# Turning the activations with DMA transposes in a fused conditional-mix and quantized-FFN kernel

## The chip, the cores and the metric

The kernel runs on one core of a Trainium2 chip. The metric is the device time of one execution in microseconds; lower is better. The kernel before was timed three times: 110.67, 111.22 and 111.39 us, median 111.22 us.

## The reference

```
w   = cond_weights[itok]                        # gather: 64 rows of a [200, 64, 64] table
y   = einsum('bct,bcd->bdt', x, w)              # x is [64, 64, 512] f32
a   = mxfp4_quant_dequant(y)                    # blocks of 32 along the 512 columns
W   = mxfp4_quant_dequant(ffn_weight)           # [512, 512]
out = x + (a @ W.T + bias)
```

`mxfp4_quant_dequant` takes the largest magnitude of each block of 32, makes a power-of-two scale from its exponent, rounds the scaled values to the e2m1 grid and scales back. All values that it gives are exact in bf16.

## The kernel before, in words

**Tiling.** Two batches of x make one tile of 128 partitions by 512 columns (32 tiles). Four tiles make a group; the code calls the work on a group a step, and there are 8 steps (`STEPS = LAST = 8`). Step 0 stands for the weight W, which goes through the same quantization.

**What one step does.** TensorE multiplies each x tile with a block-diagonal 128x128 matrix `mix` (`mix_tile`, line 252; two table rows are loaded into its diagonal blocks by `load_mixes`, line 157, one DMA of 16 KB for each) into PSUM `y_ps`. ScalarE reads y twice: magnitudes to `z` in bf16 (`z_tile`, line 356) and the value to `y_sb` in f32 (`y_tile`, line 364). VectorE reduces z to a block maximum (lines 460 to 477), makes the grid's scales from it (483 to 504, the last of them `inv`), rounds (`round_y`, line 512), limits (`limit`, line 524, which needs ScalarE's `zone`, line 372) and rescales to the quantized bf16 activations `a2` (`rescale`, line 533). The matmul with W needs the activations with k on the partitions. So TensorE transposes a2 with an identity matrix, 16 blocks of 128x128 a step (`turn_tile`, line 265), into the banks of `o_ps`; ScalarE copies them to `aT` in SBUF (`copy_turned`, line 389), and TensorE multiplies (`ffn_tile`, line 276, after a bias matmul of three partitions, `bias_tile`, line 270). Of the four output tiles in `o_ps`, tile 0 is added to x by VectorE (`add_residual`, line 538) and tiles 1 to 3 are copied by ScalarE to `o_sb` (`copy_out`, line 380) and added to x by an accumulating DMA that GpSimd issues (line 235). In the last two steps VectorE adds all tiles.

**What sets the order.** There is no planner; each engine's program is a list written out by hand, run strictly in order, with semaphore waits. The engines are skewed: in the VectorE loop (lines 579 to 594) iteration `step` rounds and rescales group `step`, begins the maxima of group `step+1`, and between them adds tile 0 of group `step-1`. TensorE in iteration `step` multiplies group `step-1` with W, mixes group `step+2` and turns group `step`.

**The queues.** SP issues in this order: the list of conditions, x of group 1 in two halves, the second half of W, then for each group the table rows of its tiles 2 and 3 and an x load of 1 MB, down to group 8 (lines 172 to 187); only behind that come the stores of each group, each behind the wait for its sums (lines 189 to 198). GpSimd issues the bias load, the table rows of tiles 0 and 1, splits the bias into three bf16 parts (lines 218 to 224), spreads them by four DMAs (227), and then issues the accumulating DMAs. ScalarE issues the first half of W.

**The start.** VectorE clears part of `mix`, quantizes W (lines 547 to 567), then begins group 1. TensorE turns W before it mixes group 2, and ScalarE copies the turned W to `wT` (line 410) before it makes zone of group 1. TensorE runs 72 small matmuls on zeros at the very start (line 291).

Of the kernel before, what the change touches and what calls it, by code (L numbers as in the profile page):

```python
# [13 lines left out]
P = 128  # L14
# [20 lines left out]
def adaln_ffn_program(nc, x, cond, table, W, bias, out):  # L35
# [11 lines left out]
    with ExitStack() as ctx:  # L47
# [13 lines left out]
        aT = sb("aT", [P, GROUP, KC, P], BF16)  # L61
# [6 lines left out]
        bias_f = sb("bias_f", [1, 3, N], F32)  # L68
# [24 lines left out]
        upper_clear, lower_clear = sem("upper_clear"), sem("lower_clear")  # L93
# [47 lines left out]
        def o_bank(step, t):  # L141
            if step < LAST or t >= 2:
                return o_ps[:, t if step < LAST else t - 2, :]
            return y_ps[:, 2 + t, :]
# [16 lines left out]
        def _(sp):  # L161
# [41 lines left out]
        def _(pool):  # L203
            nc.gpsimd.memset(mix[C:P, 0:GROUP, 0:C], 0.0).then_inc(lower_clear, 1)
            pool.dma_start(bias_f[:, 0, :], bias.rearrange("(o n) -> o n", o=1)).then_inc(bias_in, 16)
            pool.wait_ge(cond_in, 16)
            load_mixes(pool, mybir.EngineType.Pool, pool_mix_in, 1, POOL_TILES)
            pool.wait_ge(lower_clear, 1)
            nc.gpsimd.memset(mix[C:P, GROUP:TILES, 0:C], 0.0).then_inc(lower_clear, 1)
            pool.wait_ge(lower_clear, 2)  # L210
            pool.wait_ge(ident_clear, 1)
            nc.gpsimd.affine_select(out=ident[:, :], in_=ident[:, :], compare_op=ALU.not_equal, fill=1.0,
                                    base=0, pattern=[[-1, P]], channel_multiplier=1).then_inc(ident_ready, 1)
            load_mixes(pool, mybir.EngineType.Pool, pool_mix_in, 2, POOL_TILES)


            pool.wait_ge(bias_in, 16)
            nc.gpsimd.tensor_copy(bias_b[:, 0, :], bias_f[:, 0, :]).then_inc(bias_step, 1)
            for i in range(2):
                pool.wait_ge(bias_step, 2 * i + 1)  # L220
                nc.gpsimd.tensor_tensor(bias_f[:, i + 1, :], bias_f[:, i, :], bias_b[:, i, :], ALU.subtract
                                        ).then_inc(bias_step, 1)
                pool.wait_ge(bias_step, 2 * i + 2)
                nc.gpsimd.tensor_copy(bias_b[:, i + 1, :], bias_f[:, i + 1, :]).then_inc(bias_step, 1)
            pool.wait_ge(bias_step, 5)
# [3 lines left out]
            for step in range(3, STEPS + 1):  # L229
                load_mixes(pool, mybir.EngineType.Pool, pool_mix_in, step, POOL_TILES)  # L230
# [8 lines left out]
        def _(pe):  # L239
# [15 lines left out]
            def turn_tile(step, t):  # L255
                if step == 1:
                    pe.wait_ge(wT_copied, t + 1)
                elif 1 < step < LAST:

                    if t < ADDED:  # L260
                        pe.wait_ge(added, adds_before(step - 1) + t + 1)
                    else:
                        pe.wait_ge(copied_out, (GROUP - ADDED) * (step - 2) + t - ADDED + 1)
# [5 lines left out]
            def bias_tile(step, t):  # L269
                nc.tensor.matmul(o_bank(step, t), ones[32 * t:32 * t + 3, :], bias3[32 * t:32 * t + 3, :],  # L270
                                 start=True, stop=False)

            def ffn_tile(step, t):
                pe.wait_ge(aT_ready, tiles_done(step, t))
                for c in range(KC):
                    last = nc.tensor.matmul(o_bank(step, t), aT[:, t, c, :], wT[:, c, :], start=False,  # L276
                                            stop=(c == KC - 1))
                last.then_inc(o_ready, 1)

            def ffn_group(step):  # L280

                pe.wait_ge(aT_ready, tiles_done(step, GROUP - 1))
# [10 lines left out]
            pe.wait_ge(upper_clear, 1)  # L293
# [8 lines left out]
            for t in range(GROUP):  # L302
                mix_tile(2, t)
            for step in range(1, LAST):
                if step == 2:
                    pe.wait_ge(ones_ready, 1)
                    pe.wait_ge(bias3_in, 16 * GROUP)
                if step > 1:
# [4 lines left out]
                for t in range(GROUP):  # L313
                    turn_tile(step, t)
# [4 lines left out]
            pe.wait_ge(aT_ready, tiles_done(LAST - 1, GROUP - 1))  # L319
# [18 lines left out]
            pe.wait_ge(added, adds_before(LAST - 1) + 2)  # L338
# [6 lines left out]
        def _(act):  # L345
# [36 lines left out]
            def copy_turned(step, t, n):  # L382

                act.wait_ge(t_ready, GROUP * step + (t + n if step < LAST else t // 2 * 2 + 2))
                if step < LAST:
                    turned = o_ps[:, t:t + n, :].bitcast(BF16)[:, :, 0:K]
                else:
                    turned = y_ps[:, t // 2, :].bitcast(BF16).rearrange("p (g k) -> p g k", k=K)[:, t % 2:t % 2 + n, :]
                nc.scalar.copy(aT[:, t:t + n, :, :].rearrange("p g c m -> p g (c m)"), turned).then_inc(aT_ready, n)  # L389
# [8 lines left out]
            for t in range(GROUP):  # L398
                z_tile(1, t)
                if t > 0:  # L400
                    y_tile(1, t - 1)
            y_tile(1, GROUP - 1)
            for t in range(GROUP):
                z_tile(2, t)
                if t > 0:
                    y_tile(2, t - 1)
# [5 lines left out]
            for step in range(1, LAST):  # L412
                zone_group(step)
                if step == 1:
                    y_tile(2, 3)
                else:
                    if step + 1 <= LAST:
# [8 lines left out]
                copy_turned(step, 0, 2)  # L426
                copy_turned(step, 2, 2)
# [11 lines left out]
        def _(dve):  # L439
# [104 lines left out]
            nc.vector.memset(mix[0:C, :, C:P], 0.0).then_inc(upper_clear, 1)  # L544
# [80 lines left out]
```

## Time and profile before

| | |
|---|---|
| median of the three runs | 111.22 us |
| the profiled execution, its own time | 110.9 us |
| its span in the trace | 109.2 us |
| VectorE (DVE) busy | 92.5 us |
| TensorE (PE) busy | 80.3 us |
| ScalarE (ACT) busy | 79.0 us |
| GpSimd (POOL) busy | 34.3 us |
| mean granted TensorE clock | 0.937 of full speed |

PE is TensorE's matmuls, PEld its weight loads, SPq, POOLq and ACTq are DMA issues on those engines' queues. A line number is a line of the kernel. Times are in microseconds from the start of the span; the profiled execution has 1.7 us that lie outside the span.

### The profile page before, as it was taken

To read this page: it belongs to the slowest core of one execution; us is meant where nothing else is said; L and a number is where in the kernel's file an instruction comes from. 1 tells how busy PE (TensorE), PEld (TensorE's weight loads), DVE (VectorE), ACT (ScalarE), POOL (GpSimd) and SP (SyncE) were. 2 spreads that over 40 slices of the span, in tenths; PEclk is the share of its full clock that TensorE was granted. 3 is DMA by queue.
4 is the path that set the end of the run, shared out by engine and by line. 5 is a ranking of instruction groups with operands and counts; after the bars stand their busy time and mean duration, and the time that the engine had idled before them with its cause. 6 is when DMAs were issued, how large, how long until landed. Compare 5 with 4: busy or idle time off the path is not lost.

```text
span 109.2 us, 1704 instructions
## 1 busy us (share of the span) xinstructions
PE 80.3 (74%) x440; PEld 39.9 (37%) x440; DVE 92.5 (85%) x145; ACT 79.0 (72%) x113; POOL 34.3 (31%) x55
## 2 busy tenths in 40 slices
PE   5994900299140999799969969997996994389960
PEld 4952200363010834263443435335353341324420
DVE  5245999999509986999999999999999999999970
ACT  3433298006993559999999999999999999873300
POOL 4393999846754475130030003003001100300000
PEclk9999998558985589999999999999999999999999
DMA  1996989979597510339389596938948777694995
GB/s 38 401 372 136 301 304 394 332 214 357 186 295 260 192 35 22 119 76 199 101 304 180 108 362 130 180 141 285 196 113 327 144 144 285 171 207 134 350 385 203
DMA packets 13850, 23.70 MB, mean 217 GB/s; under 512 B 3846, under 2 KB 4370, under 8 KB 13842
## 3 DMA queue, kind: packets, MB, share of 16 engines
q1 hardware_dynamic: 11506, 17.83, 46.7%
q0 software_dynamic: 2048, 5.26, 23.7%
q10 hardware_dynamic: 288, 0.52, 1.3%
q8 instruction: 3, 0.05, 0.2%
q14 instruction: 5, 0.04, 0.1%
HBM read 10.49 MB, written 8.39 MB: 173 GB/s over the span
## 4 chain that ended last, share of the span: by engine, by line
DVE 59%; PE 16%; ACT 9%; issue 6%; DMA 5%; SPq 2%; DVEq 0%; ACTq 0%
DVE n_int L512 11%; DVE top L524 10%; DVE a L533 10%; DVE low L499 7%; PE y_ps L252 6%; DMA w_sb<-in_L_ffn_weight_dram 5%; DVE inv L504 4%; PE o_ps L265 3%; DVE n_int L517 3%; PE o_ps L276 3%; ACT zone L372 3%; DVE m L460 3%; DVE amax L477 2%; DVE m L466 2%; DVE s L483 2%
## 5 line engine op out<-in xcount | busy, mean ns | idle before, releaser
L252 PE MATMUL y_ps<-x_sb,mix 128*128 128x512 f32 x64 | 32.6, 639 | 4.1 <-DMA mix<-in_L_cond_weights_dram 4.1
L276 PE MATMUL o_ps<-wT,aT 128*128 128x512 bf16 x120 | 27.5, 380 | 0.0
L356 ACT ACTIVATE z<-y_ps 128x512 bf16<-128x512 bf16 x32 | 19.1, 621 | 8.4 <-PE y_ps L252 7.8
L265 PE MATMUL o_ps<-ident,a 128*128 128x128 bf16 x128 | 10.2, 242 | 17.6 <-DVE a L533 17.6
L157 POOL DMA_DIRECT2D mix<-in_L_cond_weights_dram x32 | 17.4, 546 | 13.2 <-issue 11.9
L372 ACT ACTIVATE zone<-inv 128x2048 int16<-128x2048 int16 (+1 forms) x10 | 17.5, 1755 | 3.8 <-DVE inv L504 3.7
L512 DVE TENSOR_TENSOR n_int<-y_sb,inv 128x1024 int16<-128x1024 f32 x16 | 19.0, 1222 | 0.8
L235 POOL DMA_DIRECT2D x_sb<-o_sb x6 | 5.3, 882 | 44.8 <-ACT o_sb L380 44.8
L364 ACT COPY y_sb<-y_ps 128x512 f32<-128x512 f32 x32 | 18.5, 607 | 0.0
L252 PEld LDWEIGHTS y_ps<-x_sb,mix 128*128 128x128 f32 x64 | 12.4, 207 | 15.8 <-issue 15.0
L265 PEld LDWEIGHTS o_ps<-ident,a 128*128 128x128 bf16 x128 | 8.6, 109 | 23.9 <-DVE a L533 15.5
L276 PEld LDWEIGHTS o_ps<-wT,aT 128*128 128x128 bf16 x120 | 11.0, 98 | 14.1 <-issue 2.0
L389 ACT COPY aT<-o_ps 128x1024 bf16<-128x1024 bf16 x14 | 13.5, 1015 | 3.5 <-PE o_ps L265 3.3
L524 DVE TENSOR_TENSOR top<-zone,s 128x2048 bf16<-128x2048 bf16 (+1 forms) x10 | 12.1, 1212 | 3.7 <-ACT zone L372 3.7
L460 DVE TENSOR_TENSOR m<-z 128x1024 bf16<-128x1024 bf16 (+1 forms) x10 | 6.3, 633 | 6.5 <-ACT z L348 4.6
L533 DVE TENSOR_TENSOR a<-n_int,top 128x2048 bf16<-128x2048 int16 (+1 forms) x10 | 11.4, 1141 | 0.3
L499 DVE TENSOR_TENSOR low<-z,s 128x2048 bf16<-128x2048 bf16 (+1 forms) x9 | 10.4, 1158 | 0.0
L380 ACT COPY o_sb<-o_ps 128x1024 f32<-128x1024 f32 (+1 forms) x12 | 10.1, 844 | 0.0
L538 DVE TENSOR_TENSOR x_sb<-o_ps,x_sb 128x512 f32<-128x512 f32 x12 | 8.0, 685 | 0.5 <-PE o_ps L276 0.5
L291 PE MATMUL o_ps<-idle 128*128 128x128 bf16 x72 | 7.0, 264 | 1.2 <-DVE idle L541 1.2
L291 PEld LDWEIGHTS o_ps<-idle 128*128 128x128 bf16 x72 | 5.6, 120 | 2.5 <-issue 2.2
L504 DVE TENSOR_SCALAR inv<-low 128x2048 int16<-128x2048 int16 x9 | 6.2, 684 | 0.0
(38 smaller groups left out, 55.6 us busy)
## 6 DMA issues: line engine op xcount, KB each, us to landing
x_sb<-in_x_dram SPq DMA_DIRECT2D x7, 1024.0 KB, 6.5
x_sb<-o_sb POOLq DMA_DIRECT2D x6, 768.0 KB, 5.8
out_dram<-x_sb SPq DMA_DIRECT2D x6, 768.0 KB, 3.5
out_dram<-x_sb SPq DMA_DIRECT2D x14, 256.0 KB, 3.0
x_sb<-in_x_dram SPq DMA_DIRECT2D x2, 512.0 KB, 4.9
w_sb<-in_L_ffn_weight_dram ACTq DMA_DIRECT2D x2, 256.0 KB, 3.4
w_sb<-in_L_ffn_weight_dram SPq DMA_DIRECT2D x2, 256.0 KB, 5.7
mix<-in_L_cond_weights_dram POOLq DMA_DIRECT2D x32, 16.0 KB, 3.5
```

Of the source, the lines that this page charges most:

```text
L157: queue.dma_start(mix[half, first + i // 2, half], table[bass.ds(row, 1), :, :].rearrange("o c d -> (o c) d")).then_inc(mix_in[step], 16)
L252: nc.tensor.matmul(y_ps[:, t, :], mix[:, (step - 1) * GROUP + t, :], x_tiles(step, t), start=True, stop=True).then_inc(y_ready, 1)
L265: last = nc.tensor.transpose(t_bank(step, t)[:, c * P:(c + 1) * P], a2[:, t, c * P:(c + 1) * P], ident[:, :])
L276: last = nc.tensor.matmul(o_bank(step, t), aT[:, t, c, :], wT[:, c, :], start=False, stop=(c == KC - 1))
L356: nc.scalar.activation(blocked(z[:, step % 2, t, :]), permuted_high(y_ps[:, t, :]), ACT.Abs, scale=ZONE_GAIN).then_inc(z_ready, 1)
L364: nc.scalar.copy(blocked(y_sb[:, step % 2, t, :]), permuted(y_ps[:, t, :])).then_inc(y_copied, 1)
L372: nc.scalar.activation(zone[:, t0:t0 + n, :].bitcast(I16), inv[:, t0:t0 + n, :].bitcast(I16), ACT.Copy, bias=float(EXPONENT), scale=-1.0). ...
L389: nc.scalar.copy(aT[:, t:t + n, :, :].rearrange("p g c m -> p g (c m)"), turned).then_inc(aT_ready, n)
L499: nc.vector.tensor_tensor(by_hi(low[:, t0:t0 + n, :]), by_hi(z[:, step % 2, t0:t0 + n, :]), spread(s1[:, t0:t0 + n, :], n), ALU.max).then_ ...
L512: nc.vector.tensor_tensor(n_int[:, pair, :], y_sb[:, step % 2, pair, :], inv[:, pair, :], ALU.mult).then_inc(n_done, 1)
L524: nc.vector.tensor_tensor(by_hi(top[:, t0:t0 + n, :]), by_hi(zone[:, t0:t0 + n, :]), spread(s3[:, t0:t0 + n, :], n), ALU.min).then_inc(top ...
L533: nc.vector.tensor_tensor(flat(a2[:, t0:t0 + n, :]), flat(n_int[:, t0:t0 + n, :]), flat(top[:, t0:t0 + n, :]), ALU.mult).then_inc(a2_done, 1)
```

## The change

The transposes of groups 1 to 7 move from TensorE and ScalarE to DMA. SP issues two DMA transposes for each group, one for tiles 0 and 1 and one for tiles 2 and 3, each from `a2` (128 x 1024 bf16, 256 KB) to `aT`, which now has two buffers. They stand in SP's program behind all of the load loop, in one loop with the stores: transposes of a group, then the stores of the group before. `ffn_tile` waits for the half that it needs. `rescale` waits until the transposes of the group before have landed, since a2 has one buffer. TensorE's 16 transposes and ScalarE's two copies of a step go, except for W and for group 8.

At the start, the order changes. SP loads bias and the second half of W ahead of x of group 1. GpSimd makes the identity first, clears mix for the first two groups, issues the table rows of groups 1 and 2 back to back, clears the rest of mix (all of it, the upper half too, which VectorE did), and issues those of group 3; VectorE makes the bias parts, by four operations behind a wait for the bias, ahead of its first work on W. TensorE mixes groups 1 and 2 before it turns W. ScalarE makes zone of group 1 before the copies of W and most copies of group 2. In the last group the outputs of tiles 2 and 3 go to banks of `y_ps`.

```diff
-        aT = sb("aT", [P, GROUP, KC, P], BF16)
+        aT = sb("aT", [P, 2, GROUP, KC, P], BF16)
...
             sp.dma_start(cond_sb[:, :], cond_row).then_inc(cond_in, 16)
+            sp.dma_start(bias_f[:, 0, :], bias.rearrange("(o n) -> o n", o=1)).then_inc(bias_in, 16)
+            load_w(sp, 2)
+            load_w(sp, 3)
             for h in range(2):
                 sp.dma_start(x_tiles(1, 2 * h, 2).rearrange("p (n t) -> p n t", n=2),
                              x_dram[:, 2 * h:2 * h + 2, :]).then_inc(x_first_in[h], 16)
-            load_w(sp, 2)
-            load_w(sp, 3)
...
-            for step in range(1, STEPS + 1):
+            def store_step(step):
...
+            def turn(step, half):
+                sp.dma_start_transpose(aT[:, step % 2, 2 * half:2 * half + 2, :, :].rearrange("p t c m -> p (t c) m"),
+                                       a2[:, 2 * half:2 * half + 2, :].rearrange("p t k -> p (t k)")
+                                       ).then_inc(aT_in[half], 16)
+
+            for step in range(1, STEPS + 1):
+                if step < LAST:
+                    sp.wait_ge(a2_done, step + 1)
+                    if step > 2:
+
+                        sp.wait_ge(o_ready, tiles_done(step - 2, GROUP - 1))
+                    turn(step, 0)
+                    turn(step, 1)
+                if step > 1:
+                    store_step(step - 1)
+            store_step(STEPS)
...
             def ffn_tile(step, t):
-                pe.wait_ge(aT_ready, tiles_done(step, t))
+                if step < LAST:
+                    pe.wait_ge(aT_in[t // 2], 16 * step)
+                else:
+                    pe.wait_ge(aT_ready, t + 1)
...
             for t in range(GROUP):
                 mix_tile(1, t)
+            for t in range(GROUP):
+                mix_tile(2, t)
             pe.wait_ge(ident_ready, 1)
             pe.wait_ge(a2_done, 1)
             for t in range(GROUP):
                 turn_tile(0, t)
...
                 if step > 1:
                     ffn_group(step - 1)
                 if step + 2 <= LAST:
                     mix_tile(step + 2, 0)
-                pe.wait_ge(a2_done, step + 1)
-                for t in range(GROUP):
-                    turn_tile(step, t)
...
                 if step + 2 <= LAST:
                     z_tile(step + 2, 0)
-                copy_turned(step, 0, 2)
-                copy_turned(step, 2, 2)
...
             def rescale(step, done, rounded, t0=0, n=GROUP):
-                if step > 0 and t0 == 0:
-
-                    dve.wait_ge(t_ready, GROUP * step)
+                if step == 1:
+                    dve.wait_ge(t_ready, GROUP)
+                elif step > 1:
+
+                    for half in range(t0 // 2, (t0 + n) // 2):
+                        dve.wait_ge(aT_in[half], 16 * (step - 1))
...
+            dve.wait_ge(bias_in, 16)
+            nc.vector.tensor_copy(bias_b[:, 0, :], bias_f[:, 0, :]).then_inc(bias_step, 1)
+            dve.wait_ge(bias_step, 1)
+            nc.vector.tensor_tensor(bias_f[:, 1, :], bias_f[:, 0, :], bias_b[:, 0, :], ALU.subtract
+                                    ).then_inc(bias_step, 1)
...
```

## Rows read from the trace of the kernel before

**Rows 1.** The chain that ended last, shares of the span by engine.

```profile
DVE 59%; PE 16%; ACT 9%; issue 6%; DMA 5%; SPq 2%; DVEq 0%; ACTq 0%
```

**Rows 2.** Timeline of VectorE, one step that repeats, the last ones: start, duration, line, operation.

```profile
61.41 0.68 DVE L538 TENSOR_TENSOR x_sb<-o_ps,x_sb 128x512 f32<-128x512 f32 x1
...
63.76 1.23 DVE L533 TENSOR_TENSOR a<-n_int,top 128x2048 bf16<-128x2048 int16 x1
...
70.70 0.68 DVE L538 TENSOR_TENSOR x_sb<-o_ps,x_sb 128x512 f32<-128x512 f32 x1
...
91.64 1.23 DVE L533 TENSOR_TENSOR a<-n_int,top 128x2048 bf16<-128x2048 int16 x1
...
94.91 0.68 DVE L504 TENSOR_SCALAR inv<-low 128x2048 int16<-128x2048 int16 x1
```

**Rows 3.** Busy time in one step: engines in the columns' order, clock, DMA share.

```profile
core 0: us, PE busy (x) PEld busy (x) DVE busy (x) ACT busy (x) POOL busy (x), PEclk, DMA share, GB/s
58.53:67.82 9.29, 8.44 (x46) 3.88 (x45) 9.15 (x14) 9.16 (x14) 0.86 (x1) 1.00 0.73 198
```

**Rows 4.** The same timeline, its stalls: last the [idle before].

```profile
12.96 4.28 DVE L517 TENSOR_TENSOR n_int<-w_sb,inv 128x512 int16<-128x512 f32 x4
...
28.58 0.69 DVE L460 TENSOR_TENSOR m<-z 128x1024 bf16<-128x1024 bf16 x1 [1.00 <-ACT z L356]
...
32.81 1.23 DVE L524 TENSOR_TENSOR top<-zone,s 128x2048 bf16<-128x2048 bf16 x1 [3.09 <-ACT zone L372]
...
38.23 2.36 DVE L512 TENSOR_TENSOR n_int<-y_sb,inv 128x1024 int16<-128x1024 f32 x2
41.54 0.69 DVE L460 TENSOR_TENSOR m<-z 128x1024 bf16<-128x1024 bf16 x1 [0.94 <-ACT z L356]
42.20 0.69 DVE L538 TENSOR_TENSOR x_sb<-o_ps,x_sb 128x512 f32<-128x512 f32 x1
...
43.82 1.23 DVE L524 TENSOR_TENSOR top<-zone,s 128x2048 bf16<-128x2048 bf16 x1 [0.59 <-ACT zone L372]
```

**Rows 5.** Timeline of SP's queue: what it issues, and for how long.

```profile
0.89 0.35 SPq L172 DMA_DIRECT2D cond_sb<-in_itok_B_dram  x1
...
27.18 0.59 SPq L164 DMA_DIRECT2D x_sb<-in_x_dram  x1
29.31 2.44 SPq L157 DMA_DIRECT2D mix<-in_L_cond_weights_dram  x4
31.80 0.59 SPq L164 DMA_DIRECT2D x_sb<-in_x_dram  x1
33.93 6.42 SPq L157 DMA_DIRECT2D mix<-in_L_cond_weights_dram  x8
42.92 63.75 SPq L169 DMA_DIRECT2D out_dram<-x_sb  x20
```

**Rows 6.** Timeline of TensorE: after an idle stretch, and a step that repeats.

```profile
35.45 1.89 PE L265 MATMUL o_ps<-ident,a 128*128 128x128 bf16 x16 [4.12 <-DVE a L533]
...
65.05 1.07 PE L265 MATMUL o_ps<-ident,a 128*128 128x128 bf16 x16 [0.85 <-DVE a L533]
...
68.68 0.40 PE L270 MATMUL o_ps<-bias,ones 3*128 3x512 bf16 x4
69.00 3.63 PE L276 MATMUL o_ps<-wT,aT 128*128 128x512 bf16 x16
...
98.50 0.61 PE L265 MATMUL y_ps<-ident,a 128*128 128x128 bf16 x8 [0.66 <-DVE a L533]
```

**Rows 7.** Landing times of the DMAs of 38 to 41 us: issues, KB, us to landing.

```profile
mix<-in_L_cond_weights_dram SPq DMA_DIRECT2D x4, 16.0 KB, 1.9
```

**Rows 8.** Landing times over the whole span, the same columns.

```profile
x_sb<-o_sb POOLq DMA_DIRECT2D x6, 768.0 KB, 5.8
out_dram<-x_sb SPq DMA_DIRECT2D x6, 768.0 KB, 3.5
out_dram<-x_sb SPq DMA_DIRECT2D x14, 256.0 KB, 3.0
```

**Rows 9.** The transfers to and from x_sb, all sizes: landing times.

```profile
DMA to landing us min/median/max: 2.5/3.7/8.0
```

**Rows 10.** Timeline of SP's queue from 62 to 66 us: stores of one step.

```profile
62.03 0.90 SPq L169 DMA_DIRECT2D out_dram<-x_sb  x2
```

**Rows 11.** Timeline of GpSimd: one of six accumulating DMAs.

```profile
65.52 0.86 POOL L235 DMA_DIRECT2D x_sb<-o_sb  x1 [8.40 <-ACT o_sb L380]
```

**Rows 12.** Timeline of ScalarE: the copies of turned group 7.

```profile
93.64 1.93 ACT L389 COPY aT<-o_ps 128x1024 bf16<-128x1024 bf16 x2 [0.53 <-PE o_ps L265]
```

More of the change, by code:

```diff
@@ L141, in o_bank @@
         def o_bank(step, t):
-            if step < LAST or t >= 2:
-                return o_ps[:, t if step < LAST else t - 2, :]
-            return y_ps[:, 2 + t, :]
+            if step < LAST:
+                return o_ps[:, t, :]
+            return y_ps[:, (t + 2) % GROUP, :]
         block = ctx.enter_context(nc.Block())
@@ L203, in _ @@
         def _(pool):
[L204 to L210, printed above, removed]
             pool.wait_ge(ident_clear, 1)
@@ L213, in _ @@
                                     base=0, pattern=[[-1, P]], channel_multiplier=1).then_inc(ident_ready, 1)
+            pool.wait_ge(ident_ready, 1)
+            nc.gpsimd.memset(mix[C:P, 0:2 * GROUP, 0:C], 0.0).then_inc(lower_clear, 1)
+            pool.wait_ge(cond_in, 16)
+            load_mixes(pool, mybir.EngineType.Pool, pool_mix_in, 1, POOL_TILES)
             load_mixes(pool, mybir.EngineType.Pool, pool_mix_in, 2, POOL_TILES)
[L217 to L225, printed above, removed]
+            pool.wait_ge(lower_clear, 1)
+            nc.gpsimd.memset(mix[C:P, 2 * GROUP:TILES, 0:C], 0.0).then_inc(lower_clear, 1)
+            nc.gpsimd.memset(mix[0:C, 2 * GROUP:TILES, C:P], 0.0).then_inc(upper_clear, 1)
+            load_mixes(pool, mybir.EngineType.Pool, pool_mix_in, 3, POOL_TILES)
+            pool.wait_ge(bias_step, 4)
             for t in range(GROUP):
                 pool.dma_start(bias3[32 * t:32 * t + 3, :], bias_b[:, :, :]).then_inc(bias3_in, 16)
-            for step in range(3, STEPS + 1):
+            for step in range(4, STEPS + 1):
                 load_mixes(pool, mybir.EngineType.Pool, pool_mix_in, step, POOL_TILES)
@@ L255, in turn_tile @@
             def turn_tile(step, t):
[L256 to L263, printed above, removed]
                 for c in range(KC):
@@ L269, in bias_tile @@
             def bias_tile(step, t):
+                if 1 < step < LAST:
+                    if t < ADDED:
+                        pe.wait_ge(added, adds_before(step - 1) + t + 1)
+                    else:
+                        pe.wait_ge(copied_out, (GROUP - ADDED) * (step - 2) + t - ADDED + 1)
                 nc.tensor.matmul(o_bank(step, t), ones[32 * t:32 * t + 3, :], bias3[32 * t:32 * t + 3, :],
@@ L273, in ffn_tile @@
             def ffn_tile(step, t):
-                pe.wait_ge(aT_ready, tiles_done(step, t))
+                if step < LAST:
+                    pe.wait_ge(aT_in[t // 2], 16 * step)
+                else:
+                    pe.wait_ge(aT_ready, t + 1)
                 for c in range(KC):
-                    last = nc.tensor.matmul(o_bank(step, t), aT[:, t, c, :], wT[:, c, :], start=False,
+                    last = nc.tensor.matmul(o_bank(step, t), aT[:, step % 2, t, c, :], wT[:, c, :], start=False,
                                             stop=(c == KC - 1))
@@ L382, in copy_turned @@
             def copy_turned(step, t, n):
[L384 to L389, printed above, removed]
+                act.wait_ge(t_ready, GROUP + t // 2 * 2 + 2)
+                turned = y_ps[:, t // 2, :].bitcast(BF16).rearrange("p (g k) -> p g k", k=K)[:, t % 2:t % 2 + n, :]
+                nc.scalar.copy(aT[:, step % 2, t:t + n, :, :].rearrange("p g c m -> p g (c m)"), turned).then_inc(aT_ready, n)
             load_w(act, 0)
@@ L397, in _ @@
             zone_group(0)
-            for t in range(GROUP):
+            for t in (0, 2):
                 z_tile(1, t)
-                if t > 0:
-                    y_tile(1, t - 1)
-            y_tile(1, GROUP - 1)
+                z_tile(1, t + 1)
+                y_tile(1, t)
+                y_tile(1, t + 1)
             for t in range(GROUP):
                 z_tile(2, t)
-                if t > 0:
-                    y_tile(2, t - 1)
+            zone_group(1)
+            y_tile(2, 0)
+            y_tile(2, 1)
             for t in range(GROUP):
@@ L412, in _ @@
             for step in range(1, LAST):
-                zone_group(step)
                 if step == 1:
+                    y_tile(2, 2)
                     y_tile(2, 3)
                 else:
+                    zone_group(step)
                     if step + 1 <= LAST:
```

22 lines of the change are left out of this document (13 added, 9 removed).

## The prediction

> **What bounds the kernel now.** I began with the chain that ended last: VectorE holds 59% of it [rows 1], so a microsecond counts only where it moves VectorE. Its timeline says where. From 44 us to 95.6 us it has no stall; steps repeat every 9.29 us (61.41 to 70.70 between two residual adds [rows 2]), with 9.15 of 9.29 us busy [rows 3]. ScalarE is as full (9.16 us, TensorE 8.44), but as VectorE never waits for either there, taking work off them gives nothing by itself. All stalls in the middle of VectorE's work lie in the start: 1.00, 3.09, 0.94 and 0.59 us, 5.6 in all, each "until ScalarE" [rows 4]. That is what the reordered start can win, if nothing else holds VectorE.
>
> The third view is SP's queue, since the transposes go there. SP issues loads until 33.93 + 6.42 = 40.35 us; its first store comes at 42.92 [rows 5]. This is no wait for data: a group takes four issues of table rows (2.44 us), one of x (0.59) and, between, some 1.5 us in which SP reads the row numbers (27.77 to 29.31, 32.39 to 33.93 [rows 5]).
>
> **Removed.** Each step loses 16 TensorE transposes (1.07 us at full clock [rows 6]) and two ScalarE copies of 1 us. Between 44 and 95.6 us I cost that at nothing: VectorE's unbroken work hides it. The start wins 5.6 us of stalls, and W should arrive earlier (its loads go ahead of x); VectorE's four bias operations fall into its idle time before W's data and may use it up. I take 5.6 to 7 us: VectorE would begin rounding group 2 at some 31 to 33 us in place of 38.23 [rows 4].
>
> **Added, first: the wait for SP.** In VectorE's list the rounding of group 2 and one maximum are followed by the residual add of group 1, which needs group 1 times W, which needs the transposed group 1. Its DMA transposes stand behind SP's whole load loop, which the change does not shorten; it adds the bias load, 0.4 us (the condition load issues in 0.35 [rows 5]). So SP reaches them at 40.35 + 0.4 = 40.75 us, however early group 1 is quantized.
>
> Then comes L, the time from SP's release to the landing of the first half (256 KB). The trace has no DMA transpose. Below it is bounded by the table rows, 1.9 us for 16 KB on idle queues [rows 7], and by the plain 256 KB store, 3.0 us [rows 8]; above by the slowest transfer on x_sb, 8.0 us [rows 9]. Nearest is the store of the same size; with something for short pieces and issue I take 3.5 on idle queues (38 to 43 us is idle), and 3.0 and 6 to 8 as ends.
>
> After landing, TensorE runs four bias matmuls and four of W: (69.00 − 68.68) + 3.63 / 4 = 1.23, about 1.3 us at full clock [rows 6]. It will have stood idle for over 10 us. After 4.12 us of idleness 16 transposes took 1.89 us where they take 1.07 in a running step [rows 6], the clock's lower level; I take twice 1.3, 2.6 us.
>
> The add thus starts at 40.75 + 3.5 + 2.6 = 46.85 in place of 42.20 [rows 4], +4.65. The 0.59 us stall behind it vanishes, since zone is long made: **+4.1 us**. The whole gain of the start (VectorE arrives by 34 to 36 us) is spent in a wait of 11 us or more. One more 0.5 us I allow once, because group 1's matmuls at the low clock delay the mix of group 4 and the ScalarE work behind it.
>
> **Added, second: each step.** From the end of rescale (63.76 + 1.23 = 64.99) to the add of that group (70.70) are 5.7 us [rows 2]. Today's path (transposes, copies, rest of the mixes) lets the W matmuls start at 68.68, 3.7 us after [rows 6]. Afterwards they start at L. It costs VectorE nothing while L + 1.3 < 5.7, that is L < 4.4. Queued behind the transposes on SP are only stores, which nobody but the end waits for. Ahead and beside them lie 1 MB of stores and 768 KB of accumulation a step: SP's stores issue until 62.93 [rows 10], two microseconds before the release at 65, and take 3.5 us to land; the accumulation is issued at 65.52 [rows 11] and takes 5.8 [rows 8]. The DMA engines are 0.73 busy [rows 3]; 512 KB more, at the rate of today's mixture (198 GB/s at a share of 0.73 is 271 GB/s), is 1.9 us of 9.29, a share of 0.20, so 0.93 in all: they fit, with queueing. I take L = 4.8 in a step: 0.4 us for each of the five adds of groups 2 to 6, **+2.0 us**. Rescale must also wait for the second half of the group before, 8.1 us after that was released (9.29 − 1.23): covered up to a landing of 8 us.
>
> **Added, third: the end.** Group 7 is rescaled at 91.64 + 1.23 = 92.87 [rows 2]. Bias and two tiles times W (0.3 and half of 3.63 us [rows 6]) then keep TensorE until 92.87 + L + 2.1, and it turns group 8 at 98.50 today [rows 6]; from there to the end TensorE and the adds behind it are the path. It comes late by L − 3.5: with 4.8, **+1.3 us**. ScalarE's copies of group 7 end at 95.57 [rows 12], no later than inv of group 8 (94.91 + 0.68 = 95.59 [rows 2]), on which zone waits: taking them off gives nothing.
>
> **Sum**, against the profiled execution's own 110.9 us (0.3 under the median of 111.22): 110.9 + 4.1 + 0.5 + 2.0 + 1.3 = **118.8 us**.
>
> With L = 3.0 throughout and a warm TensorE: the add at 45.05, +2.3 net, steps 0, end 0: 113.2. With L = 6: +6.6, 0.5, 5 x 1.6 = 8.0, 2.5: 128.5.
>
> On L the trace is silent beyond these rows. The Trainium skill (DMA: Bandwidth & Descriptors, "Latency and other measured facts") gives a DMA transpose 261 GB/s; by it 256 KB is 1.0 us over the 1.9 us of the table rows, an estimated 2.9, and the sum would be about 113. No row here shows it.
>
> **Rivals.**
> *Slow transposes.* Each half lands 8 us after release, the slowest row's value. Then +8.6 at the start, 0.5, 5 x 3.6 = 18.0, and 4.5 at the end: 142.5 us. For it: transposing is by short pieces, and 16 KB in short pieces took as much as 1.9 us. Against: those 1.9 are mostly fixed, as 256 KB took 3.0. The Trainium skill (VectorE: DVE Perf Modes, "The three transpose paths") puts a DMA transpose of 128x128 at 1309 ns against 390 on TensorE and prefers TensorE where PSUM will do; eight in a row would be an estimated 10.5 us for a half and 21 for a group, which would set the step in place of VectorE and bring the time over 180 us. No row shows that; I give it 0.03 of this rival's chance.
>
> *SP held by the accumulation.* Before it turns the next group, SP waits for the accumulating DMA to store. Today that lands about 2.5 us before the release [rows 2, 10]. If the transposes beside it and the later W matmuls cost it over 2.5 us, SP reaches the next transposes late, by one more microsecond a step: 118.8 + 6 = 124.8 us.
>
> *Faster: the loads do not hold the transposes.* If SP's load loop ended by 30 us, the first add would not wait and the start's gain would stay: 110.9 − 7.1 = 103.8 us. It decides from 42.20 − 0.59 − 3.5 − 1.3, so SP would have to be through by 36.8 us. Against: SP waits for nothing there that comes sooner, and the change removes no issue.
>
> *No change.* The same by halves: SP through at 37 us and fast transposes, 110 to 112 us.
>
> **Chances.** Forecast with L from 3 to 6: 0.67. Slow transposes 0.12. SP held 0.13. Faster 0.05. No change 0.03. The range takes in the forecast's bounds and the SP rival, 113 to 129; outside are 0.12, 0.05 and 0.03. A measurement of this kernel tells about 1% from no change. Faster 0.05, same 0.03, slower 0.92.
>
> **What would show it.** SP's first transpose issue at about 40.8 us, with a2 of group 1 written by 31 us at the latest. A VectorE stall of over 10 us ahead of the first residual add, which starts near 46.9. Stalls ahead of line 538 in each later step, near 0.4 us, by the W matmuls. No TensorE line 265 between W and group 8. The clock low over 20 to 44 us. The prediction is wrong if SP issues transposes before 37 us, if rescale and not the add is what waits (then the second half's landing is the price), or if a step's length stays 9.29 us (then L is under 4.4 and the time near 115).

## The result

The changed kernel takes 126.14 us (median of four runs, 125.02 to 127.74) against 111.06 us (110.67 to 111.39): a ratio of 1.133, 95% interval 1.123 to 1.142. It is slower by 15 us, inside the predicted range, and about twice the predicted 7.6. The profiled execution is the slowest of the four, 127.74 us; its differences are taken against the 110.9 us of the one before. Here and below a median is of all runs of a kernel, and a ratio of those within 1.5% of its fastest.

The chain that ended last, first two lines of that part of the page:

```profile
SPq 26%; PE 25%; DMA 20%; issue 12%; DVE 10%; ACT 4%; ACTq 0%; DVEq 0%
DMA aT<-a 20%; PE o_ps L287 15%; SPq L158 14%; SPq L154 6%; PE y_ps L262 5%; DVE a L540 4%; SPq L165 3%; ACT zone L379 3%; PE y_ps L287 3%; DVE n_int L516 2%; PE y_ps L267 1%; ACT y_sb L371 1%; DVE low L503 1%; SPq L178 1%; PE y_ps L278 1%
```

In this kernel line 203 is the DMA transpose, 287 the matmul with W, 545 the residual add and 540 the rescale. VectorE's 59% [rows 1] is now 10%. SP's queue, TensorE and the DMA transposes hold 71% of the chain; VectorE is as busy as before (92.6 us) but waits. Its stalls, from its timeline (last, in brackets, the idle time before):

```profile
31.97 2.36 DVE L516 TENSOR_TENSOR n_int<-y_sb,inv 128x1024 int16<-128x1024 f32 x2
...
45.81 0.69 DVE L545 TENSOR_TENSOR x_sb<-o_ps,x_sb 128x512 f32<-128x512 f32 x1 [10.88 <-PE o_ps L287]
...
55.04 0.68 DVE L545 TENSOR_TENSOR x_sb<-o_ps,x_sb 128x512 f32<-128x512 f32 x1
...
69.42 0.69 DVE L545 TENSOR_TENSOR x_sb<-o_ps,x_sb 128x512 f32<-128x512 f32 x1 [4.71 <-PE o_ps L287]
...
78.65 0.69 DVE L545 TENSOR_TENSOR x_sb<-o_ps,x_sb 128x512 f32<-128x512 f32 x1
...
91.21 0.69 DVE L545 TENSOR_TENSOR x_sb<-o_ps,x_sb 128x512 f32<-128x512 f32 x1 [2.76 <-PE o_ps L287]
...
100.50 0.68 DVE L545 TENSOR_TENSOR x_sb<-o_ps,x_sb 128x512 f32<-128x512 f32 x1
...
111.09 0.69 DVE L540 TENSOR_TENSOR a<-n_int,top 128x1024 bf16<-128x1024 int16 x1 [2.27 <-DMA aT<-a]
...
122.80 0.69 DVE L545 TENSOR_TENSOR x_sb<-y_ps,x_sb 128x512 f32<-128x512 f32 x1 [0.17 <-PE y_ps L287]
```

The rounding of group 2 begins at 31.97 in place of 38.23 [rows 4], so the start did gain 6.3 us. Then the first residual add waits 10.88 us. The adds of groups 3 and 5 wait 4.71 and 2.76 us, those of 2, 4 and 6 not at all. Against the adds before (42.20, 52.12, 61.41, 70.70, 80.00, 89.29 and the last at 105.63 us) they come 3.6, 2.9, 8.0, 8.0, 11.2, 11.2 and at last 17.2 us late. So the loss has three parts: about 2.9 us at the start, 8.3 in the steps, 6.0 at the end.

SP's queue, where one line holds the issues that follow each other (second column, from the first one's start to the last one's end):

```profile
34.56 6.41 SPq L158 DMA_DIRECT2D mix<-in_L_cond_weights_dram  x8
41.02 10.92 SPq L203 DMA_TRANSPOSE aT<-a  x4
51.99 6.42 SPq L170 DMA_DIRECT2D out_dram<-x_sb  x2
58.94 7.08 SPq L203 DMA_TRANSPOSE aT<-a  x2
66.06 1.06 SPq L170 DMA_DIRECT2D out_dram<-x_sb  x2
72.96 2.59 SPq L203 DMA_TRANSPOSE aT<-a  x2
75.59 6.53 SPq L170 DMA_DIRECT2D out_dram<-x_sb  x2
82.68 4.04 SPq L203 DMA_TRANSPOSE aT<-a  x2
...
94.76 2.59 SPq L203 DMA_TRANSPOSE aT<-a  x2
97.40 6.33 SPq L170 DMA_DIRECT2D out_dram<-x_sb  x2
104.03 4.49 SPq L203 DMA_TRANSPOSE aT<-a  x2
```

SP's loads end at 40.97 and group 1 is turned from 41.02, though a2 of group 1 was finished at 29.1. The pairs of groups 4 and 6 (72.96, 94.76) take 2.6 us to issue; those of 3, 5 and 7 (58.94, 82.68, 104.03) follow within 0.6 us of a 768 KB store (58.03 + 0.38, and so on) and take 7.1, 4.0 and 4.5 us. The accumulating DMA alternates with them: GpSimd issues it 0.3 to 0.5 us behind the start of the pairs of groups 3, 5 and 7 (59.44, 83.18, 104.33), and 2.2 and 1.6 us behind those of 4 and 6 (75.19, 96.36). Landing times, first of the window from 41 to 44.5 us (group 1), then of 58 to 68.2 us (group 3, with its neighbours):

```profile
aT<-a SPq DMA_TRANSPOSE x2, 2.8
```

```profile
out_dram<-x_sb SPq DMA_DIRECT2D x2, 768.0 KB, 4.4
x_sb<-o_sb POOLq DMA_DIRECT2D x1, 768.0 KB, 7.0
...
aT<-a SPq DMA_TRANSPOSE x2, 7.8
```

### The profile page after: what moved, and what is told of

It is laid out like the page before. It is cut to its first block, busy times and chain, and to the rows that moved or that the text cites. A ratio compares the mean times of both kernels' runs of the same rounds, so it can differ in the third digit from the quotient of the medians.

```text
span 126.0 us, 1465 instructions
## 1 busy us (share of the span) xinstructions
PE 82.9 (66%) x324; PEld 36.2 (29%) x328; DVE 92.6 (74%) x149; ACT 66.2 (53%) x99; POOL 28.7 (23%) x50
## 2 busy tenths in 40 slices
DMA packets 28604, 27.37 MB, mean 217 GB/s; under 512 B 18599, under 2 KB 19123, under 8 KB 28596
## 4 chain that ended last, share of the span: by engine, by line
SPq 26%; PE 25%; DMA 20%; issue 12%; DVE 10%; ACT 4%; ACTq 0%; DVEq 0%
DMA aT<-a 20%; PE o_ps L287 15%; SPq L158 14%; SPq L154 6%; PE y_ps L262 5%; DVE a L540 4%; SPq L165 3%; ACT zone L379 3%; PE y_ps L287 3%; DVE n_int L516 2%; PE y_ps L267 1%; ACT y_sb L371 1%; DVE low L503 1%; SPq L178 1%; PE y_ps L278 1%
## 5 line engine op out<-in xcount | busy, mean ns | idle before, releaser
L287 PE MATMUL o_ps<-wT,aT 128*128 128x512 bf16 x108 | 33.4, 471 | 30.1 <-DMA aT<-a 29.7
L262 PE MATMUL y_ps<-x_sb,mix 128*128 128x512 f32 x64 | 33.9, 677 | 7.3 <-ACT y_sb L371 4.2
L287 PEld LDWEIGHTS o_ps<-wT,aT 128*128 128x128 bf16 x112 | 12.4, 117 | 49.0 <-DMA aT<-a 30.2
L545 DVE TENSOR_TENSOR x_sb<-o_ps,x_sb 128x512 f32<-128x512 f32 x10 | 6.8, 687 | 20.6 <-PE o_ps L287 20.6
L262 PEld LDWEIGHTS y_ps<-x_sb,mix 128*128 128x128 f32 x64 | 13.5, 217 | 23.6 <-issue 22.0
L158 POOL DMA_DIRECT2D mix<-in_L_cond_weights_dram x32 | 17.2, 540 | 10.0 <-issue 8.7
L540 DVE TENSOR_TENSOR a<-n_int,top 128x2048 bf16<-128x2048 int16 (+1 forms) x10 | 11.2, 1119 | 2.5 <-DMA aT<-a 2.3
L528 DVE TENSOR_TENSOR top<-zone,s 128x2048 bf16<-128x2048 bf16 (+1 forms) x10 | 11.1, 1113 | 0.7 <-ACT zone L379 0.7
L393 ACT COPY aT<-y_ps 128x512 bf16<-128x512 bf16 (+1 forms) x3 | 2.1, 730 | 9.0 <-PE y_ps L267 9.0
L508 DVE TENSOR_SCALAR inv<-low 128x2048 int16<-128x2048 int16 x9 | 6.8, 756 | 0.0
L278 PE MATMUL o_ps<-bias,ones 3*128 3x512 bf16 x28 | 3.5, 385 | 1.2 <-ACT o_sb L387 1.2
L487 DVE TENSOR_SCALAR s<-amax 128x256 int16<-128x256 int16 (+1 forms) x10 | 4.1, 411 | 0.3
```

Of the source, the lines that this page charges most:

```text
L158: queue.dma_start(mix[half, first + i // 2, half], table[bass.ds(row, 1), :, :].rearrange("o c d -> (o c) d")).then_inc(mix_in[step], 16)
L262: nc.tensor.matmul(y_ps[:, t, :], mix[:, (step - 1) * GROUP + t, :], x_tiles(step, t), start=True, stop=True).then_inc(y_ready, 1)
L287: last = nc.tensor.matmul(o_bank(step, t), aT[:, step % 2, t, c, :], wT[:, c, :], start=False, stop=(c == KC - 1))
L528: nc.vector.tensor_tensor(by_hi(top[:, t0:t0 + n, :]), by_hi(zone[:, t0:t0 + n, :]), spread(s3[:, t0:t0 + n, :], n), ALU.min).then_inc(top ...
L540: nc.vector.tensor_tensor(flat(a2[:, t0:t0 + n, :]), flat(n_int[:, t0:t0 + n, :]), flat(top[:, t0:t0 + n, :]), ALU.mult).then_inc(a2_done, 1)
```

## The experiments

Two questions were open: what held the start, and why transposes that land in 2.8 us on idle queues land after 6.8 to 8.5 us for every second group. The kernel before gave 111.5 to 111.7 us beside them.

**1. Transposes ahead of the last loads.**

```diff
-            for step in range(3, STEPS + 1):
+            for step in range(3, 6):
                 load_mixes(sp, mybir.EngineType.SP, sp_mix_in, step, SP_TILES)
...
                     turn(step, 1)
+                if step + 5 <= STEPS:
+                    load_mixes(sp, mybir.EngineType.SP, sp_mix_in, step + 5, SP_TILES)
+                if step == 1:
+                    load_x(8)
```

> SP issues the transposes of group 1 ahead of the table rows of groups 6 to 8 and x of group 8; everything else is the changed kernel. If the start was lost to SP's load loop, the first residual add (45.81 us in the changed kernel) starts at about 35, since a2 of group 1 is written at 29.1 and the first half lands 2.8 us after its issue, and VectorE's 10.9 us stall goes; time 126 - 11 = 115 us. If something else held the first W matmuls (the bias spread by DMA, the copies of W), the add stays near 45 and the time at 126. The later stalls (4.7 and 2.8 us before every second add, and the end) should remain in both theories.

Measured: 116.88 us (115.07 to 120.11). The first add:

```profile
35.46 0.69 DVE L549 TENSOR_TENSOR x_sb<-o_ps,x_sb 128x512 f32<-128x512 f32 x1 [0.49 <-PE o_ps L291]
```

It stalls 0.49 us and comes 10.35 us earlier. So what held the start was the place behind SP's load loop. The later stalls remain in another form (landing times now 2.8, 4.9 and 8.1 us, minimum, median, maximum).

**2. Stores a group later.**

```diff
-                if step > 1:
-                    store_step(step - 1)
+                if step > 2:
+                    store_step(step - 2)
```

> Only the place of the stores changes: those of group s-2 are issued behind the transposes of group s, so that no 768 KB store stands ahead of the transposes on SP's queue; the accumulating DMA still runs beside them. Theory A (the transposes of groups 3, 5 and 7 land after 7 to 9 us because they stand in the queue right behind a 768 KB store): each half lands in about 3 to 4 us, the stalls before every second add (4.7 and 2.8 us) go, and the end loses its 5 us wait; 126 - 7.5 - 5 = about 113 to 114 us. Theory B (they are slow because the accumulating DMA uses the same engines): landing stays at 6 to 8 us and the time at 124 or more. The first add stays at 45.8 in both.

Measured: 119.93 us (118.84 to 121.57). No add of groups 2 to 6 waits, but rescale waits 0.3 to 1.6 us, four times, for halves of the group before, and the slowest half still lands after 7.6 us. Neither theory as I had put it: the store accounts for some 6 of the 12 to 13 us.

**3. The reordered start alone.** The `turn` loop goes from SP; the transposes by TensorE, the copies by ScalarE and their waits are those of the kernel before.

> The reordered start alone: all transposes are made by TensorE and copied by ScalarE as in the kernel before. In the changed kernel VectorE began rounding group 2 at 31.97 against 38.23 us. If the gain of the start is real and was only spent on the wait for SP, this gives 111 - 6.5 to 7 = about 104 us with a step of 9.29 us. If the start is only fast because TensorE and ScalarE have no transposes of group 1 to make, 107 to 109 us.

Measured: 106.57 us (105.26 to 106.92), ratio 0.950 (0.939 to 0.960). The start is worth 5 us by itself. The expected 104 was missed by what its end lost: the last add comes 18.1 us behind the add of group 6, where it was 16.3. Two stretches of the end show why, columns as in [rows 3]:

```profile
88.00:92.00 4.00, 2.37 (x18) 0.94 (x15) 3.90 (x7) 3.78 (x4) 0.79 (x1) 0.61 0.75 150
92.00:96.00 4.00, 4.00 (x18) 1.81 (x17) 3.76 (x7) 0.94 (x2) 0.00 (x0) 0.53 0.64 187
```

TensorE was idle 1.7 and 1.6 us about the transposes of group 7, and its granted clock went to the lower level, 1.2 GHz (0.61 and 0.53, the column ahead of the DMA share), just for the last groups. The kernel before has the same two idle times and kept 1.00 through them:

```profile
92.92 1.07 PE L265 MATMUL o_ps<-ident,a 128*128 128x128 bf16 x16 [1.71 <-DVE a L533]
95.62 0.39 PE L270 MATMUL o_ps<-bias,ones 3*128 3x512 bf16 x4 [1.63 <-ACT aT L389]
```

So the idle times by themselves do not settle it, and why the clock fell here and not there is open.

**4. Both moves of SP's program.** The edits of 1 and 2 together.

> Both moves of SP's program together: transposes ahead of the last loads, stores a group later. If the two waits are all that the DMA transposes cost, no VectorE stall is left, the step is 9.29 us, and the time is about 103 to 104 us, the same as with TensorE's transposes and the new start: then relieving TensorE and ScalarE gives nothing of its own. If the transposes cost more beside the loads and accumulation, 106 to 110 us.

Measured: 123.46 us, from 113.62 to 126.96: the fastest run is faster than any of experiments 1 and 2, the slowest slower than all of them. In the profiled run (126.21 us) one half landed after 16.8 us. Its DMA activity from 60 us on (share of the 16 engines and GB/s are the last columns; a share over 1 means that packets overlap in the record):

```profile
60.00:64.00 4.00, 3.97 (x14) 1.93 (x15) 3.90 (x7) 2.81 (x5) 0.54 (x1) 1.00 0.77 265
64.00:68.00 4.00, 1.69 (x8) 0.39 (x6) 2.98 (x4) 3.48 (x5) 0.33 (x1) 1.00 1.27 160
68.00:72.00 4.00, 3.42 (x8) 1.03 (x8) 1.53 (x3) 1.24 (x3) 0.00 (x0) 0.58 1.33 67
72.00:76.00 4.00, 0.14 (x1) 0.00 (x0) 0.83 (x2) 0.00 (x0) 0.00 (x0) 0.93 1.19 49
```

From 68 to 76 us the engines read as over 100% busy and move 67 and 49 GB/s; from 60 to 64 us, mostly stores, they moved 265. In flight from 68 us on were a transpose half, the accumulating DMA (issued at 63.46, landed after 17.5 us) and also the two stores issued behind the transposes from 64.91 (17.1 and 15.0 us). This pointed at the accumulation without isolating it.

**5. DMA transposes with the old start.** The kernel before, with the `turn` loop and its waits as in the change, and nothing of the start's reordering.

> DMA transposes as in the change, but with the start of the kernel before (W's loads, bias parts, order of TensorE and ScalarE). The transposes of group 1 stand behind SP's loads in either case, so the start should be worth nothing here: first residual add at 45 to 46 us, time 125 to 127 us as with the whole change. If the reordered start helps beside the transposes, this is slower than 126 by up to 6 us.

Measured: 127.2 us (122.93 to 129.63), no slower than the whole change beyond this spread. The first add starts at 45.36 us against 45.81. As long as SP holds the transposes, no gain of the new start is seen.

**6. Without the 768 KB stores.**

```diff
                     sp.wait_ge(x_added[step % 2], 16 * ((step + 1) // 2))
-                    store(step, ADDED, GROUP - ADDED)
```

> Leaves out the 768 KB stores of tiles 1 to 3 of groups 1 to 6; the accumulating DMAs stay where they are, and SP still waits for them. Theory A (the store ahead on SP's queue delays the transposes): every half lands in 2.8 us, no stall of over 1 us before the adds, 126 - 13 = about 113 us. Theory B (the accumulating DMA beside the transposes delays them): halves of 5 to 8 us remain, and the time is over 118 us.

Measured: 120.59 us (two runs); halves land after 2.7, 2.8 and 7.3 us (minimum, median, maximum). With the store away, as with the store later, about 6 us go and some slow halves stay. The accumulating DMA was issued 0.1 to 0.5 us behind the start of the pairs of groups 3, 5 and 7 here too, and the adds of groups 2 to 6 come at an even 9.2 to 9.9 us.

**7. Without the accumulation, the store directly ahead.**

```diff
+                    if step > 2:
+                        store(step - 2, ADDED, GROUP - ADDED)
                     turn(step, 0)
                     turn(step, 1)
...
-                pool.dma_start(x_tiles(step, ADDED, GROUP - ADDED), o_sb[:, step % 2, :, :]...
```

> Leaves out the accumulating DMAs (tiles 1 to 3 of groups 1 to 6 come out without the added part) and sets each 768 KB store directly ahead of the transposes of the group two later on SP's queue, the worst place for theory A. Theory A: the first half lands at 2.8 plus the store's 2 to 3 us, 5 to 6 us each, so a stall of about 1 us before each add, and 119 us or more. Theory B: without the accumulation the transposes pass at full rate; landing at most 5 to 6 us with a regular step, never 7 or more, and no alternation between groups; time 114 to 119. The start (45.8 us) stays.

Measured: 119.63 us (two runs). Even in the worst place behind the store no half takes over 4.7 us, and the adds of groups 3 to 6 wait 0.4 to 0.8 us, every one of them: no alternation. The time is theory A's, the landing times lie below A's and within B's, so both causes have a part. ScalarE's and SP's waits for the accumulating DMA go with it, here and in experiments 8 and 9.

**8. Neither.** Stores a group later and no accumulation.

> Leaves out the accumulating DMAs and issues the stores a group later: nothing is ahead of the transposes on SP's queue and no accumulation beside them. With one of the two taken away the kernel took 119.9 and 119.6 us and steps of about 9.8 us. If the two together make the delay: all halves in 2.7 to 3 us, steps of 9.29 us, no wait before the adds after the first, 116 to 118 us, and the rest over 111 is the wait for SP and the end. If a third cause remains, steps stay at 9.6 or more.

Measured: 113.76 us (two runs), less than expected. The landing times of the transposes, `after` meaning the changed kernel, then 2 (no store ahead), 7 (no accumulation), 8 (neither):

```profile
DMA to landing us min/median/max: 2.7/2.8/8.5
```

```profile
DMA to landing us min/median/max: 2.7/2.9/7.6
```

```profile
DMA to landing us min/median/max: 2.7/3.6/4.7
```

```profile
DMA to landing us min/median/max: 2.7/2.8/2.9
```

With both gone all 14 land in 2.7 to 2.9 us, and the steps are 9.2 us (one 9.6). The accumulation alone costs some 6 us (119.9 against 113.8), the store ahead alone as much (119.6), both together 12: with spreads of up to 3 us in these kernels, they add up. In the steps the very long landings go with the accumulation (7.6 us without a store ahead, 7.3 in experiment 6); the store ahead brings at most 4.7.

**9. Neither, and the transposes early.** The edits of 1 and 8.

> As the kernel before this one, and with the transposes ahead of the last loads: all three waits taken away. The fourth kernel of the first set differs by the accumulating DMAs alone; it took 113.6 to 127 us, with a half that landed after 16.8 us. If the accumulation makes that, this is regular (spread under 2 us) and takes 104 to 106 us, what the reordered start gives with TensorE's transposes (106.6), and no less, as VectorE sets the step. If the loads beside the early transposes make it, a spread and waits of some us remain.

Measured: 106.76 us (106.48 to 109.06), 0.8 us over the expected range, with a spread of 2.6. So the earlier place is worth 113.8 − 106.8 = 7.0 us. One wait stayed: the first add stalls 2.77 us, since the two halves of group 1 took 6.6 and 7.2 us. They stood right behind a 1 MB load of x in SP's queue, with table rows being loaded from GpSimd's queue beside them, and no accumulating DMA exists in this kernel:

```profile
27.56 0.59 SPq L165 DMA_DIRECT2D x_sb<-in_x_dram  x1
28.52 5.03 SPq L202 DMA_TRANSPOSE aT<-a  x2
```

So landings of 7 us are not the accumulation's alone. The time equals that of TensorE's transposes with the same start (experiment 3, 106.57), and that kernel still has its accumulation. In the steps where nothing waits the adds are 9.23 us apart, against 9.29 in experiment 3: relieving TensorE of 16 transposes and ScalarE of two copies is worth under 0.1 us a step, as VectorE sets it.

**10. Transposes and accumulation kept apart.**

```diff
+                    if step > 2:
+                        sp.wait_ge(x_added[step % 2], 16 * ((step - 1) // 2))
                     turn(step, 0)
...
+                pool.wait_ge(aT_in[0], 16 * (step + 1))
+                pool.wait_ge(aT_in[1], 16 * (step + 1))
                 pool.dma_start(x_tiles(step, ADDED, GROUP - ADDED), ...
```

> Early transposes and late stores as in the fourth kernel of the first set, but the accumulating DMA of a group and the transposes of the next are kept from running at the same time by waits both ways (GpSimd waits for the transposes, SP for the accumulation). Theory B: all 14 transposes land in 2.7 to 4 us and the spread of the times, 113.6 to 127 us in the kernel without these waits, shrinks to 1 or 2 us; the step is the sum of the two, about 4.2 + 6 = 10.4 us, longer than VectorE's 9.3, so 111 to 115 us. If the spread has another cause, it stays.

Measured: 121.75 us (121.62 to 122.14). The spread of 13 us is gone, and the median landing is 2.8 us (one half at 7.5, in the stretch of the loads, ahead of the first accumulation): this fits the overlap as the cause of the spread. The time was missed by 7 us: the later steps alternate between 10.1 and 12.0 us. The waits of GpSimd and of SP say what the chain is:

```profile
POOL x_sb L254 <- DMA aT<-a: 64.6, 6, 11.6
SPq L214 <- DMA x_sb<-o_sb: 28.5, 5, 8.5
```

All six accumulating DMAs waited for transposes, and five of the pairs of transposes for an accumulating DMA, so nothing else lies between them. What I had too small are the two terms: from the start of a pair to the accumulation behind it 4.7 to 6.2 us (4.2 expected), and from there to the next pair 6.0 to 7.7 (6).

**11. ScalarE issues the transposes.** The `turn` calls move from SP to ScalarE, where the copies had been; nothing else.

> The DMA transposes are issued by ScalarE, where it made the copies before, and SP is left with loads and stores as in the kernel before. So they wait neither for SP's load loop nor in a queue with the stores, but share the engines with stores, loads and accumulation. If the queue order is what costs: first residual add by 36 to 37 us, halves of 3 to 4 us, 107 to 109 us (ScalarE pays 2.6 us of issuing a step for 1.9 us of copies). If sharing the engines with the accumulation costs: halves of 5 us and more, times that spread over several us, 112 to 120.

Measured: 127.17 us (126.68 to 134.95), ratio 1.146 (1.134 to 1.158). Both expected times failed, that of queue order by most; the landing times and the spread are those of sharing the engines with the accumulation. The first add starts at 37.79 us. The landing times, and one pair on ScalarE's timeline:

```profile
DMA to landing us min/median/max: 2.7/6.7/9.6
```

```profile
55.63 5.55 ACTq L383 DMA_TRANSPOSE aT<-a  x2
61.23 1.57 ACT L350 ACTIVATE z<-y_ps 128x512 bf16<-128x512 bf16 x3 [5.02 <-issue]
```

The median landing is 6.7 us, though no store stands ahead in this queue. The longest, 9.6, is a half of group 1, beside the loads and ahead of any accumulating DMA. And when the transfers are slow, the issue is: the pair took 5.55 us, and ScalarE's own work for group 5 stood behind it for 5.02.

**12. The start alone, with TensorE kept busy.** The kernel of 3, and

```diff
+                if step == LAST - 1:
+                    pe.wait_ge(y_copied, tiles_done(LAST, 0))
+                    for c in range(16):
+                        nc.tensor.matmul(y_ps[:, 0, 0:P], idle[:, :], idle[:, :], start=True, stop=True)
                 pe.wait_ge(a2_done, step + 1)
                 for t in range(GROUP):
                     turn_tile(step, t)
```

with 16 more behind the transposes.

> The reordered start with TensorE's transposes (106.57 us, 0.950 of before), plus 32 small matmuls on zeros in TensorE's idle time before and behind the transposes of group 7. There the granted clock had fallen to its lower level from about 88 to 96 us, and the end took 18.1 us from the add of group 6 to the last add against 16.3 in the kernel before. If the clock stays up, the end is 16 to 16.5 us again and the time about 105 us; if the clock falls regardless, 106.5.

Measured: 103.57 us (102.58 to 106.33), ratio 0.929 (0.921 to 0.937), the fastest of all. The same two stretches of the end:

```profile
88.00:92.00 4.00, 2.73 (x21) 1.36 (x22) 3.76 (x5) 2.41 (x3) 0.00 (x0) 1.00 0.88 174
92.00:96.00 4.00, 4.00 (x26) 1.93 (x24) 3.90 (x7) 2.08 (x3) 0.00 (x0) 1.00 0.64 239
```

The clock stays at its upper level, 2.4 GHz (1.00). The gain over experiment 3 is 3 us, more than the 1.6 expected. In the profiled runs the end is 16.3 us against 18.1, 1.8 of it and as forecast. The start was another 1.7 us ahead (first add at 35.05 against 36.71 us), and 1.5 of that is already there at the rescale of W (16.13 against 17.66), where the two programs are the same: it is no gain of the added matmuls (the last section has what lay beside it).

## Why the prediction was right, and where its sizes were off

**Right in the sum by some luck.** 126.1 us lies in 113 to 129, but the way up differs: 2.9 us at the start where I had 4.6, 8.3 in the steps where I had 2.0, 6.0 at the end where I had 1.3. The range reached so far up because of L = 6 for every group and of SP held by the accumulation, and neither came to pass.

**What bounds the kernel: right** for the kernel before and wherever nothing waits: work taken off the other engines gave under 0.1 us a step (experiments 3 and 9). In the changed kernel the transposes of groups 3 and 5 set the step instead.

**The start's own gain: right.** 6.3 us at the rounding of group 2, where I had 5.6 to 7.

**The wait for SP: right.** SP reached the transposes at 41.02 (predicted 40.75), L was 2.8 (3.5), the first add started at 45.81 (46.85) after a stall of 10.88 us ("11 us or more"). From landing to the add it was 1.9 us and not 2.6: the clock was low as foreseen (0.52 from 34.9 to 43.8 us), but the bias matmuls had already run at 32.30. The net term came out at 2.9 us, against 4.1 + 0.5. Experiments 1 and 9 show the cause: with the transposes ahead of the last loads the stall is 0.5 and 2.8 us, against 10.9 in the changed kernel.

**Each step: the mechanism half right, the size wrong.** This is the step that failed, as put: "I take L = 4.8 in a step: 0.4 us for each of the five adds of groups 2 to 6, +2.0 us". It measured 8.3. I had listed both causes, stores ahead and accumulation beside, and the store's place within the step. But I had made one mean share of them (0.93 of the engines, "they fit, with queueing"), as if transfers shared engines without loss and every group alike. What the runs show is that L is 2.7 to 2.8 us where the transposes meet neither and 6.8 to 8.5 where they meet both, and that the cases alternate: behind a late group the store is out of the way in time, and its copies are late too, so that the accumulating DMA is issued 1.6 to 2.2 us behind the next transposes, and only 16 of its packets have moved when these are through (72.9 to 77 and 94.7 to 98.9 us). So L was either well inside the cover of 4.4 us or far outside it, and the mean of the two was no guide. The formula for the cost held: with the first halves' 8.5 and 6.8 us it gives 4.1 + 2.4 = 6.5 of the 8.3 us.

**The end: same cause.** I had L − 3.5 = 1.3 us. Group 7 is one of the slow ones, and VectorE's rescale of group 8 had to wait too, until 111.09. From the chain that ended last, in order of time:

```profile
104.03 7.03 DMA aT<-a
...
111.11 1.03 PE o_ps L287 x2
...
112.36 2.34 PE o_ps L287 x5
```

With L = 7.03 my formula gives 3.5 us; 6.0 was measured. The other 2.5 us lie in TensorE's work behind the landing. It had waited 6.6 us and ran the last two groups in part at the lower level (0.50 from 108 to 116 us), which the formula had left out although I had counted it at the start. No run separates the clock from the rest here.

**The signs.** SP's first transpose, a2 of group 1 (29.1 us) and the stall ahead of the first add came as named, and TensorE made no transposes between W and group 8. The stalls of 0.4 us ahead of each later add did not: there were two, of 4.71 and 2.76 us, and groups 2, 4 and 6 had none. The clock was only partly low early on (0.75 from 20 to 30 us, 0.82 to 34.9).

**The rivals.** "Slow transposes" did not hold in general (2.8 us by themselves), nor did the 1309 ns for a block of 128x128 of the Trainium skill (VectorE: DVE Perf Modes, "The three transpose paths") hold as a price for blocks in a row: eight landed in 2.8 us. The 261 GB/s of the Trainium skill (DMA: Bandwidth & Descriptors, "Latency and other measured facts") agrees with a half that meets nothing: 2.9 us by the estimate, 2.8 measured. "SP held by the accumulation" did not come to pass, by 0.3 to 0.6 us: the store of group 1 was issued by 58.41, and a2 of group 3 released SP at 58.94. But SP's wait for the accumulation is what put that store directly ahead of the transposes. "Faster" would have needed SP through by 36.8; in experiment 9 it was, and that still only reached 106.8 with the accumulation left out.

**Open.** Why transposes and the accumulating DMA slow each other so is not shown; alone a half lands in 2.8 us and, in the kernel before, the accumulating DMA in 5.8. Whether it is the accumulating or only 768 KB on a second queue is not settled either: no run sets a plain DMA of that size in its place, and beside loads the halves of group 1 took 6.6 to 9.6 us ahead of any accumulation (experiments 4, 9, 10 and 11). Nor did I try to split the accumulation in smaller DMAs.

## What to carry to other kernels

Work that moves to a queue starts behind everything that the queue's program lists before it: read the issuing engine's timeline to its end before counting on an early start. Don't add a transfer by its mean share of the engines: look at what is in flight in the very microseconds in which it will run, and at its slowest landing. And when the bounding engine is full, as VectorE here, keep the part of a change that removes its stalls (the start) and drop the part that relieves others.

## What the runs showed of the hardware

- A DMA transpose of 128 x 1024 bf16 within SBUF takes SP 1.3 us to issue and lands 2.8 us after its issue began, when nothing else is in flight (41 to 44.5 us of the changed kernel). Its 256 KB moved as some 1,050 packets under 512 B (18,599 of them in the changed kernel against 3,846, over 14 transposes), at about 290 GB/s while they flowed.
- Beside an accumulating DMA of 768 KB the same transfer took up to 7.6 us (experiment 2), with a 768 KB store ahead as well 6.8 to 8.5. In one run it took 16.8, with two stores also in flight, the engines reading as busy and moving 49 to 67 GB/s. With a plain 768 KB store ahead in the queue and no accumulation it took at most 4.7; right behind a 1 MB load, with table rows loading beside it, 6.6 and 7.2 (experiment 9).
- The issue itself stretches when the transfers are slow (up to 4.7 us for one in the changed kernel, against 1.3), so it holds its engine: that is 5 us of ScalarE's own work in experiment 11.
- While GpSimd did f32 and bf16 arithmetic (13.0 to 19.8 us in the kernel before), VectorE's rounding of W took 4.28 us [rows 4]; in the changed kernel, where GpSimd only issued DMAs at that time, the same four instructions took 2.50 (the overlap is all that ties the two; it was not tried by itself):

```profile
13.91 2.50 DVE L521 TENSOR_TENSOR n_int<-w_sb,inv 128x512 int16<-128x512 f32 x4
```

- Clearing has such an overlap too. In experiment 3 a VectorE instruction on 128x128 int16 that ran into GpSimd's clearing of `mix` (from 10.34 us, for 1.40) took 1.82 us and ended within 0.1 us of it; in experiment 12 the same one ran just ahead of it and took 0.23. That is where their timelines part by the 1.5 us; it was not tried by itself either:

```profile
10.00 1.82 DVE L481 TENSOR_SCALAR s<-amax 128x128 int16<-128x128 int16 x1
9.66 0.23 DVE L488 TENSOR_SCALAR s<-amax 128x128 int16<-128x128 int16 x1
```
